# Graph network with attention and experts on one Trainium2 core: banks of the second layer's first skip products, and which engine makes four low halves of weights

## What is computed

```python
h0 = x
h = gat_conv(x, edge_index, W1, a_src1, a_dst1, b1, HEADS, HID, True)     # 4 heads x 256
h = layer_norm(h, g1, be1)
h = jax.nn.relu(h)
h = h + (h0 @ Wr1 + br1)                                                   # skip of the first layer
h1 = h
h = gat_conv(h, edge_index, W2, a_src2, a_dst2, b2, 1, OUT_DIM, False)     # 1 head x 768
h = layer_norm(h, g2, be2)
h = h + (h1 @ Wr2 + br2)                                                   # skip of the second layer
return h
```

## Time and profile before

| what | us |
|---|---|
| median of 3 runs | 2356.36 |
| lowest and highest run | 2348.95, 2357.61 |
| span of the profiled execution | 2339.4 |
| TensorE busy in it | 2098.0 (90%) |
| VectorE busy | 1425.1 (61%) |
| ScalarE busy | 921.5 (39%) |
| GpSimd busy | 409.7 (18%) |
| mean granted TensorE clock | 0.952 of full |

### The profile page before, as it was taken

One profiled execution on the slowest core, in us unless ns is written; L12 is line 12 of the kernel. 1 busy time (PEld: TensorE's weight loads), 2 busy tenths in 40 slices (PEclk: granted clock), 3 DMA queues, 4 the chain that ended last, 5 costly groups with the idle time before them and its releaser, 6 DMA issues. The chain is left out here.

```text
span 2339.4 us, 32242 instructions
## 1 busy us (share of the span) xinstructions
PE 2098.0 (90%) x12766; PEld 2016.4 (86%) x12766; DVE 1425.1 (61%) x2279; ACT 921.5 (39%) x1220; POOL 409.7 (18%) x220
## 2 busy tenths in 40 slices
PE   6998999999999999999779859788888968999994
PEld 5898999998999999999759749678888947999994
DVE  7654555655762233333569863358985676888895
ACT  2342255555431111111137623125522225777672
POOL 1674200001203344433010023110020020000001
PEclk9999999999999999999869979899999978999997
DMA  6222233334330111110169851110121037999995
GB/s 220 43 49 65 93 132 115 116 115 145 119 125 21 61 46 57 52 50 1 55 241 337 275 196 61 48 45 28 64 87 62 1 151 276 368 370 362 374 365 196
DMA packets 158239, 326.89 MB, mean 140 GB/s; under 512 B 14376, under 2 KB 99336, under 8 KB 158090
## 3 DMA queue, kind: packets, MB, share of 16 engines
q1 hardware_dynamic: 133354, 265.66, 32.6%
q10 hardware_dynamic: 18976, 43.31, 5.3%
q0 software_dynamic: 5760, 15.86, 2.2%
HBM read 278.22 MB, written 46.49 MB: 139 GB/s over the span
## 5 line engine op out<-in xcount | busy, mean ns | idle before, releaser
L651 PE MATMUL banks<-weight_hi,xt_hi 128*128 128x384 f32 (+2 forms) x2208 | 741.0, 336 | 54.6 <-DVE xt_lo L1431 14.3
L654 PE MATMUL banks<-weight_lo,xt_hi 128*128 128x384 f32 (+2 forms) x2208 | 725.1, 328 | 0.0
L655 PE MATMUL banks<-weight_hi,xt_lo 128*128 128x384 f32 (+2 forms) x2208 | 724.5, 328 | 0.0
L651 PEld LDWEIGHTS banks<-weight_hi,xt_hi 128*128 128x128 f32 x2208 | 425.0, 192 | 66.7 <-issue 24.2
L654 PEld LDWEIGHTS banks<-weight_lo,xt_hi 128*128 128x128 f32 x2208 | 425.1, 193 | 0.4 <-issue 0.2
L655 PEld LDWEIGHTS banks<-weight_hi,xt_lo 128*128 128x128 f32 x2208 | 424.4, 192 | 0.0
L1896 DVE TENSOR_TENSOR weight_lo<-weight_raw,weight_hi 128x2304 fp32r<-128x2304 f32 (+2 forms) x153 | 340.2, 2241 | 58.1 <-ACT weight_hi L1159 57.8
L1159 ACT ACTIVATE weight_hi<-weight_raw 128x2304 fp32r<-128x2304 f32 (+2 forms) x153 | 287.2, 1885 | 114.7 <-DMA weight_raw<-L_ffn_w_in 47.2
L854 POOL TENSOR_TENSOR weight_hi<-weight_raw,columns 128x2304 fp32r<-128x2304 f32 x20 | 80.5, 4027 | 689.6 <-DMA weight_raw<-L_gnn_root_in 322.6
L1659 DVE TENSOR_TENSOR held_lo<-banks,held_hi 128x384 fp32r<-128x384 f32 x80 | 44.6, 558 | 213.0 <-ACT held_hi L1086 213.0
L2512 PE MATMUL banks<-held_hi,a_rel 128*128 128x384 f32 (+1 forms) x550 | 171.5, 340 | 2.8 <-ACT a_rel L1101 2.8
(11 more groups left out here) (404 smaller groups left out, 3537.2 us busy)
## 6 DMA issues: line engine op xcount, KB each, us to landing
weight_raw<-L_ffn_w_in SPq DMA_DIRECT2D x102, 1152.0 KB, 7.5
weight_raw<-L_gnn_W_in SPq DMA_DIRECT2D x32, 1152.0 KB
weight_raw<-L_ffn_W_in SPq DMA_DIRECT2D x17, 1152.0 KB, 12.3
products<-bias_rows SPq DMA_DIRECT2D x80, 192.0 KB, 1.9
slot_in<-slot_rows ACTq DMA_DIRECT2D x34, 384.0 KB, 5.4
slot_out<-bias_rows ACTq DMA_DIRECT2D x34, 384.0 KB, 7.0
weight_raw<-L_ffn_W_in SPq DMA_DIRECT2D x17, 576.0 KB, 9.6
product_back<-products SPq DMA_DIRECT2D x10, 960.0 KB, 4.6
```

Of the source, the lines that this page charges most:

```text
L651: ins = pe.matmul(dst, s[0], m[0], start=start, stop=False)
L654: pe.matmul(dst, s[0], m[1], start=False, stop=False)
L655: return pe.matmul(dst, s[1], m[0], start=False, stop=stop)
```

## The change

In the second layer the first seven skip products (j=0 to 6) take banks 0, 1, 4, 5, 6, 7 and 0 in place of 0 and 1 in turn; from j=7 on banks 0 and 1 alternate. Each product waits only for the last product in its own bank. Before the transposes of tile 0 TensorE waits for the adds of products 0 to 3, and behind them for the adds up to product 5.

The low halves of U_SKIP[0]+2, U_SKIP[0]+3, U_XL[1] and U_XL[1]+1 are made by VectorE in place of GpSimd: after skip_row(1), after skip_row(3), after skip_row(12), and after the first row tile of the second layer's xl. On ScalarE the high half of U_SKIP[0]+2 moves ahead of the square roots of tiles 3 and 4.

```diff
+        SKIP_BANKS = [0, 1, 4, 5, 6, 7]
+        def skip_bank(j):
+            return SKIP_BANKS[j % 6] if j < SKIP_FIRST else (j + 1) % 2
...
             lows(U_XL[0], 2)
-            pool.wait_ge(unit_ready, U_SKIP[0] + 2)
-            lows(U_SKIP[0] + 2, 2)
-            lows(U_XL[1], 2)
             after_phase(pool, 6)
...
+                unit_hi(U_SKIP[0] + 2)
                 for t in range(3, TILES):
                     tile_std(t)
-                unit_hi(U_SKIP[0] + 2)
                 unit_hi(U_SKIP[0] + 3)
...
                         xl_chunk(0, u, t)
-                        if u > 0 and t == 0:
+                        if layer == 1 and t == 0:
                             unit_lo(U_XL[1] + u + 1)
...
-                    vec.tensor_tensor(into, into, ps[:, j % 2, 0:GCOL], ALU.add).then_inc(prod_used, 1)
+                    vec.tensor_tensor(into, into, ps[:, skip_bank(j), 0:GCOL], ALU.add).then_inc(prod_used, 1)
...
                 skip_row(1)
+                unit_lo(U_SKIP[0] + 2)
                 begin(FULL)
                 skip_row(2)
                 finish(3)
                 skip_row(3)
+                unit_lo(U_SKIP[0] + 3)
                 finish(FULL)
                 for j in range(FULL, heads * TILES):
                     skip_row(j)
+                    if j == 2 * TILES + 2:
+                        unit_lo(U_XL[1])
...
-                        pe.wait_ge(prod_used, PR_SKIP[1] + j - 1)
+                        same = [i for i in range(j) if skip_bank(i) == skip_bank(j)]
+                        if same:
+                            pe.wait_ge(prod_used, PR_SKIP[1] + same[-1] + 1)
...
-                        ins = mm3(pe, ps[:, j % 2, 0:GCOL], at(act_t, slice(None), m, slice(t * P, (t + 1) * P)), at(w, slice(None), k), k == 0, k == kd - 1)
+                        ins = mm3(pe, ps[:, skip_bank(j), 0:GCOL], at(act_t, slice(None), m, slice(t * P, (t + 1) * P)), at(w, slice(None), k), k == 0, k == kd - 1)
...
                         skip_product(j)
+                    pe.wait_ge(prod_used, PR_SKIP[1] + 4)
                     weights_t(0)
+                    pe.wait_ge(prod_used, PR_SKIP[1] + 6)
```

## The result

The changed kernel's median is 2338.98 us (10 runs, 2333.31 to 2343.51), that of the kernel before 2349.03 us (10 runs, 2339.75 to 2357.61; three of them are those known before the prediction). The ratio is 0.9949, with a 95% interval of 0.9935 to 0.9963. The changed kernel is faster by 12.0 us by the ratio (8.7 to 15.3), by 10.0 us between the medians; the forecast was 6.7 us. Compared twice more, each time beside the kernel before on one chip, the same kernel gave 0.9962 (0.9949 to 0.9975) and 0.9947 (0.9928 to 0.9966).

What follows compares the result with a forecast made beforehand. TensorE, busy 90% of the span, was taken to wait in two stretches for GpSimd's low half and VectorE's adds. Terms 0.5 - 0.2 + 6.4 = 6.7 us off 2356.36 gave 2349.7 us, range 2339 to 2356.

Steps and rivals of the forecast that it cites:

- the base: Whole kernel: the median of the runs before, 2356.36 us, from which the forecast gain was subtracted.
- the sum: Whole kernel: 0.5 - 0.2 + 6.4 = 6.7 us gained, bounds 3.4 to 9.6.
- Place A: End of layer one: product 12 starts 2.5 us earlier, clock takes 2.0; 0.5 us gained, bounds -0.7 to +1.0.
- the term of the clock: End of layer one: half clock after the 5.6 us wait, on products 12 and 13, costs 2.0 us.
- The stretching by GpSimd: End of layer one: GpSimd's lows lengthen two VectorE instructions by 2.78 and 3.16 us, 5.94 in all.
- nothing: End of layer one: VectorE's low of U_XL[1] after skip_row(12) costs no time, as eight banks hold the queued products.
- Seam B: First xl tiles of layer two: 0.3 us lost before the fourth; -0.2 us taken, bounds -0.4 and +0.7.
- Place C: First skip products of layer two: tile 1's transposes 7.9 us earlier, clock takes 1.5; 6.4 us gained, bounds 4.5 to 7.9.
- rival (1): Pauses in Place A and Place C bring no new half clock: 10.2 us gained, 2346.2 us; chance 0.14.
- rival (3): End of layer one: VectorE's long instructions aren't GpSimd's doing; total gain 0.8 us, 2355.6 us; chance 0.06.
- (2): Second layer: VectorE's chain binds; U_SKIP[1]+2's high half no earlier relative to its unit, 3.4 us lost, 2353.1; chance 0.10.
- (4): End of layer one: 25 us at half speed after the wait cost 12.5 us, slower at 2358.7 us; chance 0.04.

Runs made afterwards that it cites:

- low3_late: The changed kernel with the low half of U_SKIP[0]+3 after skip_row(6) in place of skip_row(3); 2329.49 us (one run).
- lows_only: The kernel before with the four low halves on VectorE and the early high half, second layer still in two banks; 2336.22 us, ratio 0.9982.
- hi_early: The kernel before with only ScalarE's high half of U_SKIP[0]+2 moved earlier, low halves still on GpSimd; 2343.3 us (one run).
- banks_only: The kernel before with only the six banks and their waits in the second layer; 2334.35 us, ratio 0.9969.
- wlo_adds: The changed kernel with U_SKIP[1]+2's halves and row sum behind tile 0's transposed weights, adds 2 to 4 before tile 3's logits; 2328.03 us, ratio 0.9941, later 0.9927.

## Why the prediction was wrong

The forecast was 2349.7 us, and 2339 to 2356; the median came out at 2338.98, just below the range. Of the 10.7 us, 7.3 are in the base: three runs of before gave 2356.36, ten gave 2349.03, and the seven new ones alone 2348.80. I took the median of three runs whose middle lay near their upper end. The other 3.4 us are the sum, 6.7 against the 10.0 between the medians. Of the 10.0 the traces account for 8.9 (10.7 where the clock doesn't fall in C); the last 1.1 are within the scatter of the runs. The 8.9 lie within the bounds of the sum, 3.4 to 9.6, so it is the base that put the median below the range. In percent, the three comparisons gave 0.51, 0.38 and 0.53; the prediction's own mark between "same" and "faster", 0.5, lies inside the interval of each.

**Place A, the step that failed:** "TensorE passes into product 10 at 1708.9 without a wait". I followed the low half and forgot the bank: product 10 takes the bank of product 2, and the low half that I had put on VectorE's list at 1.7 us stands ahead of that add. In VectorE's timeline of the kernel before the add could be read:

```profile
1710.42 0.42 DVE L2234 TENSOR_TENSOR wide_rows<-wide_rows,banks 128x256 f32<-128x256 f32 x1
```

It ends at 1710.84, and 1.7 us later is 1712.54, 3.6 us after product 9; 3.78 were measured. The pause fell ahead of product 10, not 12. The end of it was right all the same: product 12 starts 23.05 us from the entry, and my 1718.85 less 1695.81 is 23.04. The forecast 5.6 us of waiting became 3.78 + 0.18 us of waiting and 6.01 - 4.36 = 1.65 us of slow matmuls, 5.61 in all. What this changed is the term of the clock: the fall came on products 10 and 11 and ran out under the wait for the add of product 4, as it had before. I had charged 2.0 us (bounds 1.5 to 3.2) for it on products 12 and 13; its price in the changed kernel is 0, as the slow products end 0.18 us ahead of the add that product 12 needs. Only in low3_late, where that add comes 1.7 us sooner, do they cost 1.4 us. A gave 2.6 us in place of 0.5. lows_only shows it alone.

**The stretching by GpSimd** held: 1.28 and 0.42 us everywhere with GpSimd idle, and hi_early, which leaves GpSimd the work, has the stretched ones. The Trainium skill (SBUF — State Buffer, "SBUF: two separate sides") gives the lock, on VectorE's side, for instructions with two SBUF inputs or in a two-port mode. The traces agree: those stretched have two SBUF inputs, and batch statistics, which read one row, were not held up in hi_early (1.29 us for two while GpSimd worked). The prediction did not draw the consequence, that where GpSimd's instruction falls decides what it costs. For the low of U_XL[1] "nothing" held: from product 12 to the transposes that follow the last product TensorE takes 17.93 us in both kernels.

**Seam B** was forecast at -0.2. Between the first xl tile and the third the changed kernel gains 0.20, loses 0.24 and gains 0.00 us in its three traces, and lows_only gains 0.02; the pause of 0.3 us forecast ahead of the fourth is 0.11 to 0.14. banks_only, which has no edit there, loses 0.28, so this is nothing that one trace could tell from scatter, and within the bounds.

**Place C** was right in its chain and its size. Forecast were product 2 right behind the logit row, products 2 to 6 back to back (14.5 us; 14.9 measured), a wait of 1.4 us (1.39), transposes of tile 1 earlier by 7.9 us (7.74 in banks_only, 7.70 counted from the third xl tile in the changed kernel), a pause of 3.1 us ahead of them (2.81), and 1.5 us for the clock behind it (1.54 and 1.57). That this last price isn't paid in every execution was in none of the steps; only rival (1) had it as nothing. The lower bound of C was not worked out soundly: it takes 3.4 us off for two falls of the clock, but the falls read from the rows are 2.5 and 1.5, 4.0 in all, and the 2.5 set 25 matmuls against 24. The range does not hang on it, as its upper end came from rival (3).

**The rivals.** (1), a clock that brings no half clock that was not there before, at 10.2 us, is nearer to the 8.9 and 10.7 us of the traces than my forecast. In A it was right in the letter, with 2.5 us for a measured 2.6: the half clock there is the one of before, and is covered as before. In C it fell in four traces of five. (2) fell: ScalarE began the high half of U_SKIP[1]+2 right after the positive part, at 1822.36, 120.9 us from the entry, and the forecast's 1819.3 is 123.5 from the entry of before, 120.9 less A's 2.6. (3) fell with hi_early. (4) fell: the slow stretch was two products long. What the forecast got wrong is therefore one term of 2.0 us, by a wait left out, and the base of 7 us.

## What to carry to other kernels

When an inserted step removes one wait of a ring of banks, write down for every following product all of its waits, the bank as well as the operand: the pause lands on the first product whose bank lies behind the inserted step. A slow clock costs only what no later wait covers, so ask first what TensorE meets behind it. A few us in a kernel of 2340 are read from the distances between matched instructions, counted from just ahead of the change (product 12 stands at 23.04 or 23.05 us in seven of the eight traces with the changed order there), while medians of a few runs moved by 7 us with nothing changed; and the change pointed to its own continuation, as what was late next could be moved out of the way as well.

## What the runs showed of the hardware that I had not expected

The same program with the same pause of 2.8 us came back at full clock once (37 matmuls in 5.92 us) and at a granted 0.78 another time (7.62 us). Four of five traces with this pause paid, 1.5 to 1.6 us on the same matmuls, and one paid nothing. Likewise, behind a pause of 3.1 or 3.2 us ahead of the xl tiles, the kernel before had 27 matmuls in 4.74 us at 0.64, and hi_early 40 in 4.79 us at 1.00. So the length of the pause alone did not settle the price; what did is open.

GpSimd's instruction over two SBUF operands lengthened VectorE's two-operand instructions in hi_early (1.28 us to 2.92 and 4.31, both ending 1.1 us after GpSimd's end) and left batch statistics at 1.29 us for two.

Stretches that no edit touched differ by up to 13.7 us in 1700 between executions (entry at 1689.4 to 1703.0), more than all gains by trace here but that of wlo_adds (14.1 and 14.4).
